# One chip kernel for an embedding, state-space and expert tower: another turn of its four instruction queues

## What is computed

```python
h = attention(emb[x] * 16 + pos)         # per row of 256 tokens: softmax over the queries, no mask
n = layernorm(h)
# state-space mixer, 8 heads of 64, state 128, chunks of 128 tokens
z, xBC, dt = split(layernorm(n) * ln_w + ln_b) @ in_proj.T)
dt  = softplus(dt + dt_bias)             # 8 numbers for each token
xBC = silu(conv4(xBC) + conv_b)          # causal convolution with 4 taps, 768 channels
Y   = chunk scan of (xs*dt, dt*A, B, C)  # within the chunk, and from the chunk before it
y   = (Y + D*xs) * silu(z)
y   = y * rsqrt(mean(y*y) + eps) * norm_w
h   = h + (y @ out_proj.T + n)
# mixture of 8 experts, the 2 best for each token, at most 1024 tokens for each expert
v = layernorm(h)
scores = softmax(v @ w_router); slot = place of the token in its expert's list
out = h + bias + sum over the 2 of weight * (gelu(v @ w1[e]) @ w2[e])
```

## Time and profile before

| | us |
|---|---|
| median of three runs | 948.93 |
| the profiled execution | 951.88 |
| its span, first to last instruction | 950.1 |
| PE busy | 912.0 (96%) |
| DVE busy | 639.9 (67%) |
| ACT busy | 529.4 (56%) |
| POOL busy | 499.2 (53%) |
| granted TensorE clock, mean | 0.984 of full |
| fill and second half, up to the start of half 3 | 72.5 |
| 14 steady halves, 72.5 to 508.0 | 435.5 |
| drain and last half, to the first expert product at 566.6 | 58.6 |
| experts, to the last product's end at 939.3 | 372.7 |

### The profile page before, as it was taken

How to read it: one execution, slowest core, us unless ns; L and a number is a source line. 1 busy time by engine, 2 the same in 40 slices (tenths; PEclk the granted TensorE clock), 3 DMA queues, 4 the chain that set the end, 5 groups by cost and what they waited for, 6 DMA issues and landing times. The chain is left out here.

```text
span 950.1 us, 17759 instructions
## 1 busy us (share of the span) xinstructions
PE 912.0 (96%) x5850; PEld 814.0 (86%) x5850; DVE 639.9 (67%) x1690; ACT 529.4 (56%) x1094; POOL 499.2 (53%) x499
## 2 busy tenths in 40 slices
PE   5999999999999999999998979999999999999995
PEld 5888888888888888898887879999999999999995
DVE  1577898889988898889887454646464646464641
ACT  1567777677667766776776223535444544444430
POOL 6357777877678767876687331222233232323342
PEclk8999999999999999999999889999999999999998
DMA  7920111001000000000000035253534343442220
GB/s 235 324 70 8 38 35 42 24 33 33 13 22 13 23 13 22 13 24 12 13 12 15 13 105 145 48 129 66 116 70 107 83 95 95 86 106 28 23 62 33
DMA packets 48486, 58.20 MB, mean 61 GB/s; under 512 B 6289, under 2 KB 43772, under 8 KB 48449
## 3 DMA queue, kind: packets, MB, share of 16 engines
q1 hardware_dynamic: 35008, 41.23, 13.6%
q0 software_dynamic: 13440, 16.50, 10.3%
HBM read 33.62 MB, written 29.75 MB: 67 GB/s over the span
## 5 line engine op out<-in xcount | busy, mean ns | idle before, releaser
L673 POOL DMA_INDIRECT out<-ye,tok_slot x56 | 95.2, 1700 | 251.5 <-DMA out<-ye,tok_slot 111.5
L934 ACT ACTIVATE hf<-bank 128x512 f32<-128x512 f32 x128 | 79.3, 619 | 199.3 <-PE bank L1717 198.9
L1340 DVE TENSOR_TENSOR h_lo<-hf,h_hi 128x512 fp32r<-128x512 f32 x128 | 88.6, 693 | 102.9 <-ACT h_hi L936 102.8
L1715 PE MATMUL bank<-w_hi,h_hi 128*128 128x256 f32 x512 | 146.1, 285 | 0.0
L1716 PE MATMUL bank<-w_lo,h_hi 128*128 128x256 f32 x512 | 144.9, 283 | 0.0
L1717 PE MATMUL bank<-w_hi,h_lo 128*128 128x256 f32 x512 | 144.9, 283 | 0.0
L1080 DVE SCALAR_TENSOR_TENSOR xc<-bank,cw,xc 128x253 f32<-128x253 f32 (+2 forms) x288 | 128.2, 469 | 1.7
L1715 PE MATMUL bank<-xe_hi,w_hi 128*128 128x512 f32 x256 | 100.2, 391 | 0.1
L1716 PE MATMUL bank<-xe_lo,w_hi 128*128 128x512 f32 x256 | 100.0, 391 | 0.0
L1717 PE MATMUL bank<-xe_hi,w_lo 128*128 128x512 f32 x256 | 99.7, 389 | 0.0
L608 POOL DMA_INDIRECT slots_dram<-rows,slot x64 | 63.5, 992 | 67.0 <-DVE slot L1209 51.5
(11 more groups left out here) (208 smaller groups left out, 2353.4 us busy)
## 6 DMA issues: line engine op xcount, KB each, us to landing
w_raw<-w SPq DMA_DIRECT2D x16, 1024.0 KB
slots_dram<-zero_row SPq DMA_DIRECT2D x1, 8320.0 KB, 29.9
xe<-slots_dram SPq DMA_DIRECT2D x15, 520.0 KB, 3.7
out<-hb SPq DMA_DIRECT2D x16, 256.0 KB, 2.1
w_raw<-in_wT SPq DMA_DIRECT2D x1, 1288.0 KB, 6.3
slots_dram<-rows,slot POOLq DMA_INDIRECT x64
out<-ye,tok_slot POOLq DMA_INDIRECT x64, 3.8
xe<-slots_dram SPq DMA_DIRECT2D x2, 260.0 KB, 3.1
```

What stands on the lines that cost most here:

```text
L673: g.indirect_dma_start(out, bass.IndirectOffsetOnAxis(ap=tok_slot[q][:, j:j + 1], axis=0), ye[q][:, j, :], None, compute_op=ALU.add).then_ ...
L934: sc.activation(hf[m % 2][:, :], h_bank[i % H_BANKS][:, :], ACT.Gelu_apprx_tanh)\
L1340: vc.tensor_tensor(h_lo[:, m, :], hf[m % 2][:, :], h_hi[:, m, :].bitcast(F32), ALU.subtract)\
L1715: te.matmul(out_, hi, rhi, start=first_, stop=False)
```

## The change

It has these parts.

- **Fill.** The exponential of A_log, which waits for the small parameter transfers, stands behind the first scores' exponentials instead of ahead of everything; so does its negation on DVE. in_proj's weights come in two transfers with semaphores of their own, and their split into high and low parts is shared between POOL and DVE. The scaling of w_out moves behind the first gather. The numbers of identity products grow: t 3 to 4, scores 2 to 4, attend 5 to 7, hT 18 to 30, dt 8 to 12.
- **Steady halves.** All four queues get another order. On PE `to_v2T` now stands ahead of `attend`, `x_to_rows` 0 between the first two segment sums, `chunk_state` ahead of the last segment sum, `choices_before` directly behind the first `own_chunk`, and each `to_yT` and `to_xT` later. On ACT `state_inputs` stands ahead of `score_exps`, `residuals` ahead of `mixer_input`, and the squares and the softplus exponentials trade places. On DVE the gate of the first chunk comes later, slots earlier, all softplus operations stand two by two in the second convolution, the embedding behind the first, and `residual` is cut in two around the third. On POOL `gated_root`, `free_rows` and `with_bias` stand ahead of both `segment_inputs`.
- **Drain.** The back of the last batch goes ahead of the routing of the one before it. The second half of the segment inputs is made on DVE. `bs` and `ea` are first copied, and the exponential of ea comes later; the output projection is cut in two. POOL describes the rows of batch t ahead of `second_root` of batch b.
- **End.** In the last expert's first group ACT weighs two of the four output tiles, where DVE weighed all four. The block is closed with `no_gpsimd_drain=True`.

The diff, cut to its core:

```diff
@@ -380,8 +381,8 @@
-        FILL = dict(t=3, scores=2, attend=5, hT=18, dt=8)
-        DRAIN = dict(state=2, seg0=3, seg1=2, seg2=2, own=2, yT0=2, yT1=2, out=2)
+        FILL = dict(t=4, scores=4, attend=7, hT=30, dt=12)
+        DRAIN = dict(rows=2, seg0=2, rows1=8, state=6, yT1=5, out=4)
         LAST = dict(v2T=19, route=2, choices=8)
...
@@ -620,14 +627,16 @@
                         skip_x(b, q, 0)
+                        skip_x(b, q, 1)
+                        pool.wait_ge(y_ready[q], y_ready.now(b, q))
+                        with_bias(Turn(b.reg, b.shift - 1), q)
                         second_root(t, p)
-                        skip_x(b, q, 1)
+                        gated_root(b, q)
                         with_bias(t, p)
                         describe_rows(t, p)
-                        gated_root(b, q)
                         second_root(b, q)
+                        with_bias(b, q)
                     else:
-                        with_bias(t, p)
                         describe_rows(t, p)
...
@@ -640,22 +649,21 @@
                     gather_next(f, p)
+                if not b:
+                    scale_w_out()
                 if t:
...
                     scatter_rows(t, p)
+                if b:
+                    gated_root(b, q)
+                if t:
+                    free_rows(t, p)
                 if not nf:
                     segment_inputs(f, p, 0)
-                    gated_root(b, q)
-                    segment_inputs(f, p, 1)
-                    free_rows(t, p)
+                    return
+                if t:
                     with_bias(t, p)
-                    return
-                if b:
-                    gated_root(b, q)
                 segment_inputs(f, p, 0)
-                if t:
-                    free_rows(t, p)
-                    with_bias(t, p)
                 if b:
...
@@ -796,6 +801,15 @@
+            def state_copy(r, p):
+                act.wait_ge(btg_psum[p], btg_psum.now(r, p))
+                sc.activation(bs[p][:, :], bank[1 - p][3][:, 0:NS], ACT.Copy)
+                copy(ea[p][:, :], bank[1 - p][3][:, 3 * P:3 * P + NH], bs_ready[p])
+            def carry_exp(r, p):
+                act.wait_ge(bs_ready[p], bs_ready.now(r, p))
+                sc.activation(ea[p][:, :], ea[p][:, :], ACT.Exp)
             def state_inputs(r, p):
...
@@ -844,42 +858,45 @@
                     silu_z(b, q, 0)
+                    silu_z(b, q, 1)
                     silu_conv(b, q, 2)
-                    silu_z(b, q, 1)
-                    state_inputs(b, q)
+                    state_copy(b, q)
                     x_rows(b, q, 0)
...
                     x_rows(b, q, 1)
+                    carry_exp(b, q)
                     decay(b, q, 2)
...
                     state(b, q)
+                    transposed_y(b, q, 0)
+                    transposed_y(b, q, 1)
+                    squares(b, q)
                     norm_2(t, p)
                     transposed_rows(t, p)
-                    transposed_y(b, q, 0)
                     router_exp(t, p)
-                    transposed_y(b, q, 1)
-                    squares(b, q)
                     return
...
                     silu_conv(b, q, 0)
+                    silu_conv(b, q, 1)
                 if f:
...
                 if b:
-                    silu_conv(b, q, 1)
                     silu_z(b, q, 0)
...
                     silu_conv(b, q, 2)
+                    state_inputs(b, q)
                 if f:
                     score_exps(f, p)
-                if b:
-                    state_inputs(b, q)
+                if f and not b:
+                    act.wait_ge(s_small, 16 * N_SMALL)
+                    sc.activation(neg_a[:, :], alog[:, :], ACT.Exp).then_inc(s_nega, 1)
                 if t:
...
                 if b:
+                    decay(b, q, 0)
                     x_rows(b, q, 0)
-                    decay(b, q, 0)
                     decay(b, q, 1)
...
@@ -890,26 +907,23 @@
                 if b:
+                    state(b, q)
                     decay(b, q, 3)
...
                     normed(f, p)
-                if b:
-                    state(b, q)
-                if f:
+                    residuals(f, p)
                     mixer_input(f, p)
+                    last_tap(f, p, 0)
                 if b:
...
                 if f:
-                    residuals(f, p)
-                    last_tap(f, p, 0)
+                    last_tap(f, p, 1)
+                if b:
+                    transposed_y(b, q, 1)
+                    squares(b, q)
+                if f:
                     dt_exp(f, p)
-                if b:
-                    transposed_y(b, q, 1)
-                if f:
-                    last_tap(f, p, 1)
                     last_tap(f, p, 2)
-                if b:
-                    squares(b, q)
...
@@ -1215,19 +1252,24 @@
                 if b and not f:
-                    mask_scores(b, q)
+                    mask_scores(b, q, p)
+                    segment_inputs(b, q, seg_hi, a_hi)
                     times_dt(b, q, 0)
+                    segment_inputs(b, q, seg_lo, a_lo)
                     decay_scores(b, q, 0)
-                    residual(t, p)
                     times_dt(b, q, 1)
                     decay_scores(b, q, 1)
+                    residual_sum(t, p)
                     first_y(b, q)
+                    gated(b, q, 0)
                     carried_y(b, q)
+                    skipped_y(b, q)
                     second_y(b, q)
+                    residual_norm(t, p)
+                    mean_square(b, q)
+                    residual(b, q)
                     router_in(t, p)
                     router_top(t, p)
-                    mean_square(b, q)
-                    residual(b, q)
                     slots_of(t, p)
...
@@ -1254,28 +1301,32 @@
                     carried_y(b, q)
+                    gated(b, q, 0)
                 if f:
...
                 if b:
-                    second_y(b, q)
-                if f:
-                    dt_in(f, p)
+                    skipped_y(b, q)
                 if t:
                     slots_of(t, p)
-                if nf:
-                    embedded(nf, q)
-                if f:
+                if b:
+                    second_y(b, q)
+                if f:
+                    dt_in(f, p)
                     conv(f, p, 0)
...
                     count_choices(p)
+                if nf:
+                    embedded(nf, q)
+                if b:
+                    mean_square(b, q)
                 if f:
                     conv(f, p, 1)
-                if b:
-                    mean_square(b, q)
+                if b and nf:
+                    residual_sum(b, q)
                 if f:
...
                 if b and nf:
-                    residual(b, q)
+                    residual_norm(b, q)
                 if f:
...
@@ -1602,31 +1661,29 @@
                     project_z(b, q, 1)
-                    keep_clock(p, DRAIN["state"])
-                    state_inputs(b, q)
+                    state_inputs(b, q, p)
+                    keep_clock(p, DRAIN["rows"])
                     x_to_rows(b, q, 0)
...
                     segment_sums(b, q, 0)
-                    keep_clock(p, DRAIN["seg1"])
                     segment_sums(b, q, 1)
+                    keep_clock(p, DRAIN["rows1"])
                     x_to_rows(b, q, 1)
-                    keep_clock(p, DRAIN["seg2"])
                     segment_sums(b, q, 2)
                     segment_sums(b, q, 3)
+                    keep_clock(p, DRAIN["state"])
                     chunk_state(b, q)
-                    keep_clock(p, DRAIN["own"])
                     own_chunk(b, q, 0)
-                    to_v2T(t, p)
                     from_state(b, q)
-                    keep_clock(p, DRAIN["own"])
                     own_chunk(b, q, 1)
-                    keep_clock(p, DRAIN["yT0"])
                     to_yT(b, q, 0)
-                    route(t, p)
-                    keep_clock(p, DRAIN["yT1"])
+                    pe.wait_ge(y_ready[q], y_ready.now(b, q))
+                    project_rows(b, q, 0)
                     to_yT(b, q, 1)
                     keep_clock(p, DRAIN["out"])
-                    project_out(b, q)
+                    project_rows(b, q, 1)
+                    to_v2T(t, p)
+                    route(t, p)
                     choices_before(t, p)
...
@@ -1649,59 +1706,59 @@
                 if b:
-                    state_inputs(b, q)
+                    state_inputs(b, q, q)
+                if f:
+                    values(f, p)
+                if b:
+                    segment_sums(b, q, 0)
                     x_to_rows(b, q, 0)
-                if f:
-                    values(f, p)
-                if b:
-                    segment_sums(b, q, 0)
                     segment_sums(b, q, 1)
+                if t:
```

(29 more changed lines are left out.)

148 lines of the change are left out of this document (90 added, 58 removed).

## The result

| | before | after |
|---|---|---|
| median, us | 948.71 (947.77 to 952.65, 4 runs) | 966.87 (963.23 to 969.81, 4 runs) |
| ratio, with its 95% interval | 1 | 1.018 [1.0137, 1.0223] |
| the profiled execution; its span | 951.88; 950.1 | 969.81; 968.1 |
| start of half 3 | 72.48 | 69.42 |
| start of half 17 | 508.00 | 530.63 |

The direction was forecast, with a chance of 0.52 for slower; 966.87 is above the range (935 to 964) and 12.4 us above the forecast of 954.5. The spans differ by 18.0 us, and the starts in the table cut this into four: fill and second half -3.06, fourteen steady halves +25.7 (461.2 for 435.5), drain -0.4 (58.17 for 58.58), experts and end -4.2 (379.3 for 383.5).

The account below looks back on a forecast made before the run. PE was taken to bound the steady halves, busy 30.69 of 31.25 us. Terms 18.2 - 3.8 - 3.3 - 0.5 - 4.7 = +5.9 gave about 954.5 us from the median 948.93, range 935 to 964.

Parts of the forecast that it names:

- The chain in the steady halves: Steady halves: table load exposed behind bs delays rows and ohs, so PE waits: +1.3 us each, 18.2 for 14.
- the sum: Whole kernel: steady halves 18.2, fill -3.8, drain -3.3, wait ahead of the experts -0.5, end -4.7, together +5.9 us.
- one more switch: PE in steady halves: one more switch between full and rounded float32 product groups, under 0.1 us.
- The clock in the steady halves: Rival, chance 0.04: PE's clock falls with waits of 0.65 and 1.1 us; +50, about 1005, or +3, about 958.
- The drain: Drain: the 2.10 us wait and slow stretch behind it go; last scatter 3.3 us sooner, bounds 0 and -6.
- the wait before the experts: PE ahead of the experts: wait of 4.52 us shrinks to about 3, clock may hold; -0.5 us.
- Softplus two by two: DVE's second convolution: about 0.7 us longer, decay inputs a 1 to 1.2 us later, covered by slack; costed at nothing.
- nmax comes about 0.7 us sooner: DVE in steady halves: with_bias leaves its place beside lm, so nmax gains 0.7 us, unused since needed only at 8.75.
- Fill and end: Fill and second half: the 6.11 us wait goes, -3.8 us; end: POOL's DRAIN goes, -4.7 us.
- The prediction's last step: Whole kernel: from 957.8 for an execution like the profiled 951.88 to about 954.5 from the median 948.93.

Follow-up runs that it names:

- the order on ACT alone, in the kernel before: The kernel before with only ACT's state_inputs moved ahead of score_exps: 967.18 us, 1.0193.
- PE's old list: The kernel after with ACT's score_exps ahead of state_inputs again and PE's steady halves in the order of before: 982.19 us, 1.0341.
- the early table: The kernel after with a one-column exponential on ACT ahead of state_inputs, so the table load stands directly behind the last Silu: 958.36 us, 1.0098.
- the two runs of the edges: The kernel after with all queues' steady lists of before: 944.32 us; that with half 2 in new order and drain identity products moved: 939.45 us.
- undoing the ACT order: The kernel after with only ACT's score_exps put ahead of state_inputs again: 954.41 us, 1.0052.
- DVE's old list: The kernel after with ACT's score_exps ahead of state_inputs again and DVE's steady halves in the order of before: 985.97 us, 1.0398.

## Why the prediction was wrong

- **The chain in the steady halves** was right, nearly link by link. Forecast and measured, us into the half: bs 7.08 and 7.12, ea 8.66 and 8.70, rows 9.66 and 9.67, end of edec 12.46 and 12.47, to_v2T 10.80 and 10.86, own_chunk 16.24 and 16.24, ohs ready 19.09 and 19.08, second own_chunk 20.7 and 20.62. The waits were 0.56 and 0.94 for 0.65 and 1.1. The undisturbed half of 32.34 is 1.23 over the mean of before, 435.5 / 14: 17.2 us for the 18.2 of the sum. PE's busy time grew by 0.15 us a half, for the "under 0.1" of one more switch. One link held by luck: the prediction left the last Silu where it was, but it ended 0.8 us later, at 6.64, and only the 0.47 us that bs then still waited for PE kept this out of the sum.
- **The clock in the steady halves** is the step that failed. It had a chance of 0.04 and two prices, a fall in every half (+50) or around half 17 (+3). It fell in four of the fourteen, for 3.41 us each, which cost 1.67 us each; with the waits that the halves behind them then had, these halves are 8.4 us over 32.34. The price of a fall was off as well: +50 for fourteen is 3.6 us each. The argument against it, that 0.56 us of idle in every half of before left the clock alone, says nothing on 1.5 us in two pieces. With identity products in place of the idle time no fall is left in that profile. But the idle time alone doesn't tell where it falls: waits of 0.53 and 0.68 us in every half (the order on ACT alone, in the kernel before) and of 1.68 (PE's old list) left it at full, while less than 0.25 and 0.94 (the early table) had four falls. What sets them off stays open.
- **The drain** was forecast at -3.8, with the wait before the experts, and gave -0.4. The last projection ended 26.1 us into the drain, not 24.5: PE waited 1.34 us for y and ran the first half of the projection at half clock. In the profiles where the clock stayed up there, behind the same wait, it ended at 23.8 to 24.3, as costed by hand. The last rows were ready at 33.65, not 32.1, and the identity products, costed to end 1.9 us after them, ended 4.2 after: PE waited 2.23 us for ohs ahead of them and then ran them at half clock. By the two runs of the edges, with 19 of these products and with 6, some 1.4 us of this are the products' number. The rest is a wrong yardstick: the forecast took the 2.10 us wait and the slow stretch behind it for a fixed part of the old drain, whose last projection ended at 31.2. Without the slow stretch, and with the wait still there, it ended at 27.5 and the whole drain took 54.61 us. That the kernel after shows -0.4 is two slow drains compared; no gain of the new drain is shown.
- **Softplus two by two** was costed at nothing, since dt has slack. Its 0.7 us were sized right and put on the wrong consumer: nmax stands behind it in the same list. "nmax comes about 0.7 us sooner" was false; it came 0.35 later, though lm ahead of it took 0.17 us for 1.34, as costed. In the sum this costs nothing, because bs and the load end later still, but alone it is 12.8 us. It is likely a part of why undoing the ACT order gives back only part, since probs then wait for nmax; that isn't tested by itself.
- **Fill and end**: -3.06 for -3.8, with PE's waits of 1.16 us for v and 0.89 for xT, and the clock up; with DVE's old list it fell in the same fill, from 22.0 to 25.5 us behind a wait of 1.99 us for v, and half 3 started at 71.52. The end, with the experts, -4.2 for -4.7.

Sum of the misses, on the profiled execution (+18.0 for +5.9): waits -1.0, clock and what follows it +8.4, fill +0.7, drain +3.4, end +0.5, together 12.0. The prediction's last step from 957.8 to "about 954.5" is a slip too: 948.93 + 5.9 is 954.8. Still open is why the clock falls in some halves and not in others with the same waits, and how much of the runs' spread (963.23 to 969.81 us, at mean clocks of 0.991 to 0.986) is its doing.

## What to carry to other kernels

Cost a longer piece of a list by everything behind it in that list, not by who reads its result: 0.7 us of slack in dt hid nothing for the nmax behind it. Before you count a slow stretch of the old profile as a gain, see whether it is there in every execution. Where a reorder adds idle time to an engine that was dense, give a fall of its clock a real chance and its own price for "in some halves", and where fillers stand ahead of real work, compute their end from the wait ahead of them and at half clock too. An engine's list can't be judged alone: try a part of such a change with all its partners, or at the edges where it stands by itself.

## What the runs showed of the hardware

- A PE idle time of 0.93 us, with another of 0.56 some 8 us before it, was followed within 0.7 us by 3.41 us at 0.50 of the clock, in four halves of fourteen; the same idle times left the clock at full in the others.
- The length of the idle time doesn't order the falls. In fourteen steady halves the clock fell five times with waits of 0.56 and 0.77 us, four times with under 0.25 and 0.94, once with 1.36 and 0.76, and never with 0.53 and 0.68, nor with one of 1.68. Each is one profile.
- The same wait of 2.1 us in the same drain was followed by 0.55 of the clock in one execution and by 1.00 in another, and the drains took 58.58 and 54.61 us.
- With identity products in these gaps the profile has no fall in the steady halves, and the kernel took 961.33 us for 966.87, though they do nothing.
- Closing the block without POOL's DRAIN is worth 4.3 us by the ratio (0.9955 [0.9928, 0.9981]), in the kernel before, against 4.73 in the trace.
